# A two-layer attention and feed-forward kernel: the fourth weight set of the down product is issued ahead of the residual's last two quarters

## The reference

```python
def _matmul_lora(x, w, a, b, scale=1.0):
    out = jnp.einsum('bsd,hd->bsh', x, w)
    out = out + jnp.einsum('bsr,hr->bsh', jnp.einsum('bsd,rd->bsr', x, a), b) * scale
    return out
gate = _matmul_lora(x, gate_w, gate_a, gate_b)
up = _matmul_lora(x, up_w, up_a, up_b)
hidden = jax.nn.silu(gate) * up
out = _matmul_lora(hidden, down_w, down_a, down_b)
...
x = x + _L1_ffn_ref(_layernorm(x, axis=-1), ...)
```

## Time and profile before

| | us |
|---|---|
| median of 3 runs | 1185.7 |
| lowest and highest | 1184.68, 1187.55 |
| the profiled execution's own time | 1188.8 |
| its span in the trace | 1187.0 |
| TensorE busy in the span | 1091.5 (92%) |
| VectorE busy | 917.0 (77%) |
| ScalarE busy | 523.9 (44%) |
| mean granted clock of TensorE | 0.977 |

### The profile page before, as it was taken

One profiled execution on the slowest core, in us unless ns is written; L12 is line 12 of the kernel. 1 busy time (PEld: TensorE's weight loads), 2 busy tenths in 40 slices (PEclk: granted clock), 3 DMA queues, 4 the chain that ended last, 5 costly groups with the idle time before them and its releaser, 6 DMA issues.

```text
span 1187.0 us, 16323 instructions
## 1 busy us (share of the span) xinstructions
PE 1091.5 (92%) x6028; PEld 535.5 (45%) x6034; DVE 917.0 (77%) x1830; ACT 523.9 (44%) x815; POOL 155.8 (13%) x183
## 2 busy tenths in 40 slices
PE   4787999799989999969999999999999997969798
PEld 2354555644545444424444444444444443424343
DVE  8998889888983278878888988888787756455565
ACT  6896744663253324654545445443543421221211
POOL 4884430091004010000000000000001000000000
PEclk9998999899999999989999999999999997989999
DMA  9620000132032047871353524432202712122221
GB/s 370 264 88 1 2 1 1 72 109 69 1 107 85 5 118 210 208 133 72 98 144 115 151 80 134 118 105 98 96 28 80 259 45 88 44 98 72 89 80 54
DMA packets 104207, 118.44 MB, mean 100 GB/s; under 512 B 74752, under 2 KB 78976, under 8 KB 104128
## 3 DMA queue, kind: packets, MB, share of 16 engines
q1 hardware_dynamic: 104128, 117.40, 31.8%
HBM read 86.97 MB, written 16.78 MB: 87 GB/s over the span
## 4 chain that ended last, share of the span: by engine, by line
PE 61%; DVE 28%; ACT 5%; DMA 3%; issue 3%; SPq 0%; DVEq 0%; ACTq 0%
PE PAIR L2789 31%; PE PAIR L2887 13%; PE PAIR L2441 4%; PE PAIR L2443 4%; PE PAIR L2442 4%; DVE PAIR L1686 3%; DVE LORA L1685 3%; DVE LORA L1687 3%; DVE X L1734 2%; DMA STG<-in_down_w 2%; PE PAIR L2744 2%; DVE POOL L1867 1%; DVE POOL L1560 1%; PE PAIR L2648 1%; DVE BST L1532 1%
## 5 line engine op out<-in xcount | busy, mean ns | idle before, releaser
L2789 PE MATMUL PAIR<-XT,POOL 128*128 128x512 f16 x1008 | 230.9, 382 | 9.0 <-DMA XT<-POOL 5.3
L2789 PEld LDWEIGHTS PAIR<-XT,POOL 128*128 128x128 f16 x1008 | 98.4, 98 | 126.3 <-issue 13.8
L1129 ACT ACTIVATE POOL<-STG 128x512 f16<-128x512 f32 (+1 forms) x167 | 96.2, 612 | 108.7 <-DVE STG L1975 104.0
L2887 PE MATMUL PAIR<-POOL 128*128 128x512 f16 x528 | 128.5, 403 | 14.5 <-DVE POOL L1867 14.5
L2441 PE MATMUL PAIR<-POOL 128*128 128x512 f16 x336 | 128.1, 381 | 2.3 <-DVE POOL L1777 2.3
L2442 PE MATMUL PAIR<-POOL 128*128 128x512 f16 x336 | 128.0, 381 | 0.0
L2443 PE MATMUL PAIR<-POOL 128*128 128x512 f16 x336 | 128.0, 381 | 0.0
L2789 PE MATMUL PAIR<-X,POOL 128*128 128x512 f16 x504 | 115.7, 379 | 1.3 <-DMA X<-POOL 1.3
L1129 ACT ACTIVATE POOL<-ST 128x512 f16<-128x512 f32 (+1 forms) x64 | 39.5, 617 | 166.5 <-DVE ST L1862 166.5
L1867 DVE TENSOR_TENSOR POOL<-STG,POOL 128x512 f16<-128x512 f32 (+1 forms) x167 | 106.2, 669 | 1.2 <-ACT POOL L1129 1.1
L1975 DVE SCALAR_TENSOR_TENSOR STG<-STG,PAIR 128x512 f32<-128x512 f32 (+1 forms) x48 | 30.8, 642 | 94.5 <-PE PAIR L2821 72.9
(11 more groups left out here) (342 smaller groups left out, 1945.4 us busy)
## 6 DMA issues: line engine op xcount, KB each, us to landing
STG<-in_gate_w SPq DMA_DIRECT2D x21, 512.0 KB, 5.0
STG<-in_up_w SPq DMA_DIRECT2D x21, 512.0 KB, 5.7
STG<-in_ctx_t SPq DMA_DIRECT2D x16, 512.0 KB, 3.8
STG<-in_ctx SPq DMA_DIRECT2D x16, 512.0 KB, 4.2
STG<-in_down_w SPq DMA_DIRECT2D x16, 512.0 KB, 7.5
POOL<-in_ctx SPq DMA_DIRECT2D x12, 512.0 KB, 11.1
X<-in_x SPq DMA_DIRECT2D x8, 512.0 KB, 9.7
xt_keep<-POOL SPq DMA_DIRECT2D x16, 256.0 KB, 3.0
```

The source lines that it names most:

```text
L1129: e.activation(block(j, name)[:, 0, :, :], src, ACT.Copy).then_inc(b_hi, 1)
L2789: i = e.matmul(dst, blk[:, a_, k, :], src[:, b_, k, :], start=(opens and k == 0 and n == 0), stop=(k == KD // 2 - 1 and n == 2), skip_grou ...
L2887: last = e.matmul(dst, blk[:, a_, i - i0, :], src[:, b_, :], start=first, stop=(c == NSET - 1 and i == i1 - 1 and n == 2))
```

## The change

In SyncE's list, inside pass p, the loads of the residual's quarters 2 and 3 come one weight set later:

```diff
                 for d in range(NSET * p + 2, min(NSET * p + 5, CHUNKS)):
                     load_down(2 * d)
                     load_down(2 * d + 1)
-                    if d == NSET * p + 2:
+                    if d == min(NSET * p + 3, CHUNKS - 1):
                         load_sum(p, 2)
                         load_sum(p, 3)
                 send(p)
```

## The result

| | us |
|---|---|
| before, median of 4 runs | 1185.76 (1184.68 to 1187.55) |
| changed kernel, median of 4 runs | 1167.57 (1166.63 to 1168.29) |
| ratio, 95% interval | 0.9845 [0.9828, 0.9862] |
| the changed kernel's profiled execution | 1167.87, span 1166.1 |

What follows compares the result with a forecast made beforehand. TensorE and VectorE work bounds the kernel, with late fourth-set loads idling TensorE in three passes. Waiting 13.95 plus slow matmuls 4.4 gives 18.4: 1185.7 - 18.4 = 1167.3 us; own range 1164.5 to 1170.5, over the cases 1161.5 to 1172.5.

Steps and rivals of the forecast that it cites:

- the fourth set: Down product, passes 0 to 2: weight load stuck behind the residual's last quarters; issued at 958.36 instead of 975.00, its wait goes.
- The fold stretch: TensorE, third chunk of each pass: fold 0 to fold 3 falls to 6.51 us from 14.39, 12.92 and 12.16; 19.94 saved.
- The second gap: TensorE idle 4.83 us after fold 3, before the next chunk's first block product; waits for ScalarE's `first_product` and stays.
- a sign of being wrong: Behind the second idle time, 36 block matmuls took 10.45 us in pass 0; running slow for longer would refute the forecast.
- the usual run carries less half clock: Slow folds: smallest row taken for each pass, 3 x 1.48 = 4.4 us, so gain 18.4 instead of 19.9.
- What was added at no cost: Reordered loads, SyncE's extra wait and transfers beside work: zero cost taken, 0.5 us in all as upper end.
- 1, the half clock only moves: The remaining idle time takes over the slow stretches; only the waiting, 13.95 us, is won: 1171.8 us; chance 0.13.
- 2, the second gap loses its half clock: Half clock goes altogether behind the remaining idle time: gain 26.3, 1159.4 us, or 1161 to 1165 if partly; chance 0.12.
- 3, another wait at the same place: VectorE's addition also waits for fold 0 or its turn; gain under 3.6 us, some 1184; chance 0.03.
- 4, SyncE held ahead of the residual: New wait delays the residual's last quarters; costs only beyond 18 us of lateness, 1196 us at 28 us; chance 0.02.

Runs made afterwards that it cites:

- x1_pass0: Against the kernel before: fourth weight set moved ahead of the residual's last quarters in pass 0 alone, old order in passes 1 and 2; 1181.77 us, ratio 0.9936.
- x2_both: Against the changed kernel: the fifth weight set also goes ahead of the residual's last quarters; 1169.38 us, 0.9832 of before.
- x4_half: Against the changed kernel: only the fourth set's first half goes ahead of the residual's last quarters, its second half behind them; 1170.68 us, 0.9847 of before.
- x5_held: Against the changed kernel: SyncE waits for the residual's first sum before issuing the fourth set, still ahead of the quarters; 1170.09 us, 0.9870 of before.
- v1_copy_first: Against the changed kernel: ScalarE's copy of the A11 bank put ahead of the next chunk's high halves; 1166.90 us, 0.9831 of before.
- the repeat: The changed kernel run once more, unchanged, beside the kernel before; 1168.23 us, 0.9835 of before.
- x6_gap2: Against x5_held: the fourth set held instead until TensorE has finished S1 of the pass's last chunk; 1177.09 us, 0.9910 of before.

## Why the prediction was right

**The wait and its cause.** The forecast said that the fourth set was issued when it was wanted, and that its wait would go in all three passes. x1_pass0 shows it pass by pass, x2_both and x4_half that it is this set and mostly its first half. As an account of the lateness it was incomplete: it took the moment of the issue as the whole cause and the load's flight as given. x5_held shows that of some 4.5 us of lateness only 1.2 was the moment of the issue, and 3.25 the longer time to the addition behind the quarters and beside more loads. Issued 1.2 us earlier and ahead of the quarters, the set did nearly as well as with the 17 us by which the forecast moved it (975.00 against 958.4).

**The fold stretch.** Forecast 6.51 us in each pass and 19.94 in all; measured 6.51, 6.50 and 6.51, 19.95 in all.

**The second gap.** Forecast to keep its 4.83 us; it did, 14.5 us in all. That its label named the wrong engine was read from the code; v1_copy_first showed it. The cost of its slow matmuls was mis-sized by 0.17 us a pass: 10.45 and 9.62 are sums of an order of time that include the last matmul's end, the 7.77 of the earlier trace rows goes to the next start. From start to start it was 2.52, 1.68 and 1.68 us, not 2.68 and twice 1.85.

The prediction gave as a sign of being wrong that the second gap's matmuls run slow for longer than 10.45 us. That sign came: 10.66 and 10.83 us in the changed kernel, 10.71 in the repeat. It does not mean what it was to mean. The three passes' slow matmuls behind the second gap sum to 5.88 us before, 7.29 in the changed kernel and 5.94 in its repeat, and over all 27 such gaps of 4.83 us in the nine traces that have them a single one cost 1.38 to 2.89 us. The row of 10.45 was one value of that spread, not its upper end.

**From the profile to the median.** The sum of the profiled execution was 19.9, of which the forecast kept 18.4, on the ground that the usual run carries less half clock than the one profiled. The size was right (18.2), the ground is not shown, and the closeness is in part luck. The measured interval of 16.4 to 20.4 us takes in both sums, and the repeat gave 20.2. In the two traces the gap between the folds gave its whole 19.95, and the stage lost 18.5 for another reason: the second gap's slow matmuls happened to cost 1.4 us more, which the forecast had put at zero. The granted clock speaks against the ground: the profiled execution had a mean of 0.977, and of the 27 executions of the kernel before in the three groups of experiments (whose chips may be others) only two had as much (0.966 to 0.978 in all). How the four runs of the median, which have no trace, divided their time is open.

**What was added at no cost.** The loads in flight beside work cost nothing visible: the longest of the 44 additions is 0.690 us, before 0.689, and the longest load took 7.9 us to land instead of 9.1 (the tile STG of the changed kernel, 930 to 1187, ns and us, min/median/max):

```profile
L1975 DVE SCALAR_TENSOR_TENSOR STG<-STG,PAIR x44: 553/686/690, 941.8 to 1144.3; 128x512 f32<-128x512 f32 x28, 128x384 f32<-128x384 f32 x16
...
DMA to landing us min/median/max: 3.4/5.4/7.9
```

The residual's additions start without a wait.

**The rivals.** 1, the half clock only moves: it did not, 19.95 us were won between the folds. The 1.4 us more behind the second gap are not in the repeat (0.06 more), so they lie within what varies. A small shift is not excluded: over all traces such a gap cost 1.84 us on average in the 8 passes that also had the first gap, 2.08 in the 19 that did not. 2, the second gap loses its half clock: not in this kernel's two profiles, nor in any of the 27 gaps of 4.83 us; in v1_copy_first, where the gap is 3.58 us, one pass of three ran at full clock (24 matmuls in 5.34 us). 3, another wait at the same place: none. 4, SyncE held ahead of the residual: its slack of 18 us measured 17.8, and the 7.7 us of VectorE's waiting beyond it cost TensorE 1.25, where the forecast had counted all lateness beyond the slack.

## What to carry to other kernels

In a queue that is issued in order, look for a wait that holds loads which do not need it: a buffer free since 958 whose load goes out at 975 is a gain that costs nothing. How early it has to go is the flight time in the company that it will have; here the company was worth 3.25 us and the moment 1.2. Behind such a gap look for the next one, and check its label against the code: of two instructions that end at nearly the same time (here 0.13 us apart) the profile names one, and here it named the wrong one, with 20 us more behind it.

## What the runs showed of the hardware

Idle times of TensorE and the half clock (0.50, 1.2 GHz) behind them, over the down product in all thirteen traces: after 4.83 us in front of a new pass it came 27 times in 27 and cost 1.4 to 2.9 us; after 3.55 to 4.87 us before fold 1 it came eight times in eight (1.4 to 2.9 us). After 3.58 and 3.59 us in v1_copy_first it came twice in three, after 2.31 to 2.35 us in x6_gap2 once in three, after the 2.13 to 2.15 us at the mark six times in thirteen (1.6 or 1.7 us), after 1.72 us and less never. At the mark the same program gets it or not: in the changed kernel the twelve matmuls behind that idle time took 2.75 us, in its repeat

```profile
941.54 0.40 PE L2821 MATMUL PAIR<-LORA 96*128 96x128 f16 x4 [2.13 <-DVE STG L1975]
941.77 4.43 PE L2887 MATMUL PAIR<-X,POOL 128*128 128x512 f16 x12
```

Here is x6_gap2's first pass in windows of one microsecond (us of the window, PE busy and matmuls begun, granted clock, DMA share, GB/s); TensorE was busy until 979.91 and from 982.23 on:

```profile
981.00:982.00 1.00, 0.00 (x0) 1.00 1.05 395
982.00:983.00 1.00, 0.77 (x6) 0.82 0.97 294
983.00:984.00 1.00, 1.00 (x4) 0.50 1.10 395
...
986.00:987.00 1.00, 1.00 (x9) 0.97 0.27 98
```

So the same program at the same place, with idle times that agree within 0.04 us, gets the half clock in one pass and not in the next. The Trainium skill (TensorE: Matmul & The Clock Gate, Part 1) says that how many matmuls run slow varies from run to run; the traces agree (behind pass 0's gap of 4.83 us 2.72 us of slow matmuls in the changed kernel, 1.49 in its repeat), and here it varies within one run.
